# Narrow attention in 32-row products, with the last products of a step carried into the next

## The reference

```python
def _L0_xattn_ref(query, context, Wq, Wk, Wv, Wo):       # D_HEAD = 8, N_HEADS = 16
    Q = (query @ Wq.T).reshape(B, T_q, N_HEADS, D_HEAD)
    K = (context @ Wk.T).reshape(B, T_c, N_HEADS, D_HEAD)
    V = (context @ Wv.T).reshape(B, T_c, N_HEADS, D_HEAD)
    scores = jnp.einsum('bqhd,bkhd->bhqk', Q, K) / jnp.sqrt(8)
    attn = jax.nn.softmax(scores, axis=-1)
    return jnp.einsum('bhqk,bkhd->bqhd', attn, V).reshape(B, T_q, D) @ Wo.T
# _L2_xattn_ref: the same without the four weights (Q = query, K = V = context)
x = x + tanh(g_xattn[0]) * _L0_xattn_ref(layernorm(x), ctx, Wq, Wk, Wv, Wo)
x = x + tanh(g_ffn[0]) * _L0_ffn_ref(layernorm(x), ...)
x = x + tanh(g_xattn[1]) * _L1_xattn_ref(...)            # wide: 16 heads of 64
...
x = x + tanh(g_xattn[2]) * _L2_xattn_ref(layernorm(x), ctx, ctx)
...
```

## Time and profile before

| | us |
|---|---|
| time, median of 3 runs (lowest to highest) | 943.33 (939.79 to 945.34) |
| the profiled execution | 940.68 |
| its span, first to last instruction | 938.9 |
| PE matmul busy | 821.1 (87%) |
| DVE busy | 695.5 (74%) |
| ACT busy | 444.0 (47%) |
| POOL busy | 196.6 (21%) |

### The profile page before, as it was taken

One profiled execution on the slowest core, in us unless ns is written; L12 is line 12 of the kernel. 1 busy time (PEld: TensorE's weight loads), 2 busy tenths in 40 slices (PEclk: granted clock), 3 DMA queues, 4 the chain that ended last, 5 costly groups with the idle time before them and its releaser, 6 DMA issues. The chain is left out here.

```text
span 938.9 us, 14422 instructions
## 1 busy us (share of the span) xinstructions
PE 821.1 (87%) x5078; PEld 589.1 (63%) x5078; DVE 695.5 (74%) x1320; ACT 444.0 (47%) x663; POOL 196.6 (21%) x162
## 2 busy tenths in 40 slices
PE   4788878989999988999858887479999879999997
PEld 2555545667666677777646555346667567777774
DVE  6688866665766767888767888966766686887785
ACT  2245453224655514999514544145655225555553
POOL 2000010002365321222400001114554410111112
PEclk8699998987999998999968999779999989999999
DMA  9000000040101200000200060000222000000000
GB/s 363 13 1 0 1 1 1 1 179 1 42 7 46 46 1 1 1 1 0 90 0 1 1 285 1 1 1 2 46 46 47 1 1 1 0 1 0 0 1 23
DMA packets 3515, 29.48 MB, mean 31 GB/s; under 512 B 544, under 2 KB 768, under 8 KB 1920
## 3 DMA queue, kind: packets, MB, share of 16 engines
q1 hardware_dynamic: 3456, 28.70, 9.0%
HBM read 28.07 MB, written 0.62 MB: 31 GB/s over the span
## 5 line engine op out<-in xcount | busy, mean ns | idle before, releaser
L186 PE MATMUL banks<-normed_t_high,work_split 128*128 128x512 f32 x264 | 119.8, 454 | 15.5 <-DVE work L575 3.9
L889 POOL TENSOR_TENSOR work<-work 128x512 f32<-128x512 f32 x64 | 82.9, 1296 | 148.8 <-PE banks L745 106.7
L188 PE MATMUL banks<-normed_t_high,work_split 128*128 128x512 f32 x264 | 108.1, 410 | 0.0
L187 PE MATMUL banks<-normed_t_low,work_split 128*128 128x512 f32 x264 | 108.0, 409 | 0.0
L552 DVE TENSOR_REDUCE work<-banks 128x2 f32<-128x512 f32 x128 | 84.9, 687 | 27.3 <-PE banks L387 26.8
L499 ACT ACTIVATE work<-banks 128x1024 f32<-128x1024 f32 x64 | 65.3, 1024 | 47.9 <-PE banks L402 47.9
L186 PEld LDWEIGHTS banks<-normed_t_high,work_split 128*128 128x128 f32 x264 | 51.5, 195 | 37.8 <-issue 12.7
L1617 ACT ACTIVATE work<-banks 128x512 f32<-128x512 f32 x68 | 40.6, 597 | 72.1 <-PE banks L188 72.1
L1730 DVE TENSOR_TENSOR work<-work,banks 128x512 f32<-128x512 f32 x68 | 46.6, 686 | 35.3 <-ACT work L1617 34.8
L387 PE MATMUL banks<-work_split 128*128 128x256 f32 x256 | 61.0, 341 | 12.7 <-DVE work L552 10.1
L726 PE MATMUL banks<-work 128*64 128x256 f32 x512 | 69.4, 392 | 3.0 <-ACT work L856 1.7
(11 more groups left out here) (264 smaller groups left out, 1768.0 us busy)
## 6 DMA issues: line engine op xcount, KB each, us to landing
raw_b<-in_wf SPq DMA_DIRECT2D x1, 6528.0 KB, 18.1
raw_a<-in_wf SPq DMA_DIRECT2D x1, 4096.0 KB, 12.1
raw_b<-reciprocal_rows SPq DMA_DIRECT2D x6, 512.0 KB, 5.7
raw_a<-reciprocal_rows SPq DMA_DIRECT2D x6, 512.0 KB, 5.8
raw_a<-in_wf SPq DMA_DIRECT2D x1, 2048.0 KB, 13.6
raw_b<-in_wb SPq DMA_DIRECT2D x1, 2048.0 KB, 18.2
raw_a<-in_wb SPq DMA_DIRECT2D x1, 2048.0 KB, 7.3
small_operands<-in_small SPq DMA_DIRECT2D x1, 1530.0 KB, 9.1
```

The lines of the kernel that those rows point to most:

```text
L186: nc.tensor.matmul(o, w[0], m[0], start=start, stop=False)
L187: nc.tensor.matmul(o, w[0], m[1], start=False, stop=False)
L188: return nc.tensor.matmul(o, w[1], m[0], start=False, stop=stop)
L889: nc.gpsimd.tensor_tensor(w_ps[g % 2].rearrange("p (h q) -> p h q", h=2), v[:, :, 0, :], v[:, :, 1, :], ALU.add).then_inc(W["ps"].sem, 1)
```

## The change

- **Rows by selectors.** The three-term projection for each group and half is gone. In call 0 all heads are projected once, ahead of the first step (`small_project_pe`, four times `mm3`), and split into a high and a low part by ACT and DVE. In both calls `rows` then copies the 8 rows of each head of a group into their 32-row places by two products of 512 columns with matrices of zeros and ones (`a_selector`). ACT alone takes the result out of the bank (`stacked`), and adds the ones to the keys as the activation's bias. The DVE steps `stack`, `masked_keys` and the `small_weights` of each group are gone. The selectors come by two DMAs of 512 KB ahead of the bulk of the small operands (the two loads of 512 KB of repeated weights shrink to one of 128 KB), and ACT converts them to fp32r at the start of each call.
- **32-row products.** `maxima` and `scores` multiply only the 32 rows of a head (form 32 x 128), so the masked copies aren't needed. A group `u` of `scores` now covers two heads and both key halves of one batch, and its four products alternate between the two heads' row strips, into two banks; the two products of a `maxima` tile have the same head.
- **Order.** `values` goes by batch (eight products): the second batch of step `x` and the `sums_back` and `normalise` of step `x` stand inside step `x + 1`. The first batch stands behind the last `maxima`.
- **Constants.** `stream`, products of the identity with itself, stands at four places of a step of PE: nine products a step, and more ahead of the first step.
- All loops over the steps are written out. In call 1 the layernorm of the context (`context`) moves to the last step's place of the maxima on DVE, and `first_att` behind it. `sp` waits for other semaphores ahead of the loads of `wf1` and `wf3`.

```diff
-        A = signals("a", NG, w=2, q=4, hi=4, y=4, km=8, v=2, mx=16, red=16, m2=2, mt=2, yf=2, s=8, p=8, pv=8,
+        A = signals("a", NG, yp=4, y=4, v=2, mx=16, red=16, m2=2, mt=2, yf=2, s=8, p=8, pv=4,
...
+        def small_project_pe(pe):
+            pe.wait_ge(s_aw, 2)
+            for n in range(4):
+                h, k = n // 2, n % 2
...
+                mm3(bank(2 + n), [w[:, k * P:(k + 1) * P] for w in a_w], src).then_inc(s_aq, 1)
...
+            def rows(x, k):
...
+                elif k:
+                    at("y", 2 * x + 1)
+                else:
+                    at("att", x - 3)
+                hi, lo = (((xh, xl), (a_kh, a_kl)), ((xh, xl), (ch, cl)))[c][k]
+                nc.tensor.matmul(bank(a_bank(x, k)), a_selector(k, g, 0), half(hi, h), start=True, stop=False)
+                nc.tensor.matmul(bank(a_bank(x, k)), a_selector(k, g, 1), half(lo, h), start=False, stop=True)\
+                    .then_inc(A["yp"].sem, 1)
...
+            def maxima(x, n):
+                pair, j = n // GH, n % GH
...
+                at("red", 8 * x + n - 1)
+                for e in range(2):
+                    t = 4 * (x % 2) + 2 * pair + e
+                    last = nc.tensor.matmul(ps[:, 7 - n % 2, e * S:(e + 1) * S], a_y[a_rows(j), t * P:(t + 1) * P],
+                                            half(a_ky, x % 4)[a_rows(j), pair * S:(pair + 1) * S],
...
             def scores(x, u):
...
+                b = u // 2
+                at("p", 4 * x + u - 1)
+                for kb in range(2):
+                    for j in range(2 * (u % 2), 2 * (u % 2) + 2):
+                        last = nc.tensor.matmul(ps[:, j, kb * S:(kb + 1) * S],
+                                                half(a_ky, x % 4)[a_rows(j), b * S + kb * P:b * S + (kb + 1) * P],
+                                                half(a_yf, x % 2)[a_rows(j), b * S:(b + 1) * S],
...
+                more(0)
+                if x:
+                    stream(2, 4, S)
+                at("yf", x + 1)
                 scores(x, 0)
-                more(0, 1)
+                if x + 2 < STEPS:
+                    at("att", x - 1)
+                    stream(2)
+                next_rows(0)
+                more(1)
                 scores(x, 1)
                 more(2)
+                if x:
+                    values(x - 1, 1)
+                scores(x, 2)
                 more(3)
-                values(i, x, 0)
-                scores(x, 2)
-                if projecting:
-                    project(i, x + 2, 1)
+                if x + 2 < STEPS:
+                    at("y", 2 * (x + 2) + 1)
+                    stream(2)
+                next_rows(1)
                 more(4)
-                values(i, x, 1)
+                scores(x, 3)
                 more(5)
-                scores(x, 3)
+                if x:
+                    sums_back(x - 1)
                 more(6)
-                values(i, x, 2)
                 more(7)
-                values(i, x, 3)
...
+                values(x, 0)
+                if x + 1 < STEPS:
+                    stream(3, 4, S)
+                    maxima_back(x + 1)
...
+            for x in range(2):
+                rows(x, 0)
+                stream(3, 6)
+                rows(x, 1)
+                stream(3, 6)
             for n in range(8):
-                maxima(0, 0, n)
-            maxima_back(0, 0)
+                maxima(0, n)
+                stream(2)
+            stream(3)
+            maxima_back(0)
+            stream(4, 4)
```

The slots of ACT and of DVE, as they are now:

```diff
+            def slot(x):
+                weights(x, 0)
+                if x + 2 < STEPS:
+                    stacked(x + 2, 0)
+                weights(x, 1)
+                if x:
+                    sums(x - 1)
+                weights(x, 2)
+                if x + 2 < STEPS:
+                    stacked(x + 2, 1)
+                weights(x, 3)
...
+            def slot(x):
+                if x + 1 < STEPS:
+                    for n in range(8):
+                        largest(x + 1, n)
+                    minus(x + 1)
+                elif aside is not None:
+                    aside()
+                if x:
+                    normalise(x - 1)
+                if x + 1 < STEPS:
+                    queries(x + 1)
```

More of the change, by code:

```diff
@@ new lines, in small_project_act, with small_project_dve @@
+        def small_project_act(act):
+            for n in range(4):
+                act.wait_ge(s_aq, n + 1)
+                nc.scalar.activation(half((xh, a_kh)[n % 2], n // 2), bank(2 + n), ACT.Copy).then_inc(s_ah, 1)
+        def small_project_dve(dve):
+            for n in range(4):
+                dve.wait_ge(s_ah, n + 1)
+                hi, lo = ((xh, xl), (a_kh, a_kl))[n % 2]
+                nc.vector.tensor_tensor(half(lo, n // 2), bank(2 + n), half(hi, n // 2).bitcast(F32), ALU.subtract)\
+                    .then_inc(s_al, 1)
@@ new lines, in scores, with values @@
+                last.then_inc(A["s"].sem, 1)
+            def values(x, b):
+                if b == 0:
+                    at("v", x + 1)
+                    at("raw", x)
+                at("p", 4 * x + 2 * b + 2)
+                for kb in range(2):
+                    for j in range(GH):
+                        last = nc.tensor.matmul(ps[a_rows(j), 4, b * S:(b + 1) * S],
+                                                a_vg[:, 4 * (x % 2) + 2 * b + kb, j, :],
+                                                a_p[2 * b + j // 2][:, (2 * (j % 2) + kb) * S:(2 * (j % 2) + kb + 1) * S],
+                                                start=kb == 0, stop=kb == 1)
+                last.then_inc(A["pv"].sem, 1)
@@ L605, in small_dve, with slot @@
-            for x in range(2):
-                stack(0, x, 0)
-                stack(0, x, 1)
-                masked_keys(0, x)
-            small_weights(dve, c, 1, raw, r0)
+            def slot(x):
+                if x + 1 < STEPS:
[4 more added lines that the diff above has]
+                    aside()
+                if x:
+                    normalise(x - 1)
+                if x + 1 < STEPS:
+                    queries(x + 1)
@@ L610, in small_dve @@
             for n in range(8):
-                largest(0, 0, n)
+                largest(0, n)
             dve.wait_ge(s_ainit, c + 1)
-            minus(0, 0)
-            queries(0, 0)
-            with dve.Fori(0, NG - 2) as i:
-                order.loop(i, 4)
-                slot(i, 0, True, True, True)
-                slot(i, 1, True, True, True)
-            order.end(NG - 2)
-            slot(NG - 2, 0, True, True, True)
-            slot(NG - 2, 1, False, True, True)
-            slot(NG - 1, 0, False, False, True)
+            minus(0)
@@ L623, in small_dve @@
+            queries(0)
+            for x in range(STEPS):
+                slot(x)
             if before_last is not None:
                 before_last()
-            slot(NG - 1, 1, False, False, False)
+            normalise(STEPS - 1)
         def small_out_pe(pe):
@@ L1904, in context_and_first @@
                 norm_sums(dve, order, 6, 0, res)
-                for h in range(2):
-                    norm_tiles(dve, order, 5, h, ctok, ctok)
             def last_att(h):
```

329 lines of the change are left out of this document (147 added, 182 removed).

## The result

The changed kernel takes 915.19 us (median of 4 runs, 910.95 to 915.71), the kernel before 942.38 beside it: a ratio of 0.970, 95% interval 0.966 to 0.974. The profiled execution has a span of 913.0 us against 938.9. So 26 us were gained in the trace where 37.9 were forecast. Two runs of the kernels further down, one with all of the steps' constants on a strip (933.9 us) and one without the carry (966.4 us), were in a slower state at a lower granted clock; they count in the medians of the table there, but not in its ratios.

A forecast was written before the change was run, and what follows sets the result against it. DVE and PE were taken to hold each other up in a ring, neither full. Savings of 12.0 + 12.8 (steps) + 6.0 + 8.0 (starts) - 0.9 (ends) = 37.9 us took 940.7 to 903; range 878 to 930.

The forecast's parts named there:

- PE becomes the bound at 10.6 us a step: Steady steps: PE's list of products, constants and 13 form changes sums to 10.6 us, against 11.47 before.
- cheap changes: Rival, form changes: going between 32 rows and the full array costs nothing; 26 us less, 877; chance 0.14.
- no pairs: Rival, scores: 32-row products run one by one, costing 0.94 us more in 14 steps; 916; chance 0.12.
- dear changes: Rival, form changes: each costs 0.34 us, 2.2 more in 14 steps and 5 in the starts; 939; chance 0.06.
- open loads: Rival, maxima and scores: weight loads on one strip aren't hidden, 2.8 us a step; 942, no gain; chance 0.05.
- The starts, 6.0 and 8.0: Ahead of each call's first step: first queries come 6.0 us earlier in call 0 and 8.0 in call 1.
- Step 0 takes 8.3: First interval of each call: absent products and changes come off PE's list, 0.5 us wait for queries added; 8.3 us.
- The clock falls, as a rival: Rival, steps: 32-row products lower the clock, 8.3 us more a step; 1030, or 968 at half the time; chance 0.10.
- Constants mostly fill waits: Steps: most of the constants' 2.07 us isn't lost, since without them PE would wait about as long.
- No further wait: Steps: waits ahead of scores(x, 0) and maxima_back are covered by PE's other work, so 10.6 us stands.
- Ends of the calls, selectors and small operands: Call ends cost 0.9 us more together; selector copies fit ACT's idle time, and small operands' delay was taken as nothing.

The follow-up runs named there:

- all of the steps' constants on a strip: The filled kernel with all constants in the steps made 32-row products on strip 3, those ahead of the first step unchanged: 910.0 us, ratio 0.967.
- without the carry: The filled kernel with the last values and sums_back put back at the end of their own step, copy and normalise moved likewise: 960.9 us, ratio 1.023.
- the first experiment: The changed kernel with constants added in step 0 of each call, where later steps have other work: 911.1 us, ratio 0.968.
- the best kernel: The lean one, with step 0 filled, one pair of step constants on a strip, one moved and one dropped: 894.7 us, ratio 0.951.
- no constants in the steps: The changed kernel with all stream calls taken out of the steps, those ahead of the first step kept: 913.3 us, ratio 0.973.
- some constants on a strip: The changed kernel with constants between the first maxima and ahead of scores(x, 0) made 32-row products on strip 3: 906.0 us, ratio 0.965.
- the filled kernel: Same run as the first experiment: the changed kernel with nine more constants in step 0 of each call: 911.1 us, ratio 0.968.
- the one with moved constants: The filled kernel with the pair ahead of scores(x, 0) on a strip and the pair ahead of rows(x + 2, 1) moved before sums_back: 901.0 us, ratio 0.957.
- the lean one: The one with moved constants, also without the pair of constants ahead of rows(x + 2, 0): 894.7 us, ratio 0.951.
- the one with the second maximum first: The lean one with maxima(x + 1, 1) moved from behind the rows to ahead of scores(x, 0): 898.1 us, ratio 0.952.
- the bare start: The lean one without any constant ahead of the first step, those in the steps kept: 896.0 us, ratio 0.950.
- the short start: The lean one with, ahead of the first step, one constant for three behind each rows and one for two behind each maxima pair: 894.5 us, ratio 0.948.

## Why the prediction was right and where it was off

*PE becomes the bound at 10.6 us a step.* Right as to the bound: 10.44, with DVE idle for 3.8 us a step. That the number is so near is in part luck. The sum priced PE's work at 10.6 to 10.7, and it is 10.0, since `maxima` and `scores` on different strips run side by side (the rows from 62.62 on), about 0.6; the missed wait of 0.42 ahead of `sums_back` put most of it back. The prices held: pairs on two strips, loads hidden, 0.18 to 0.19 for a change of form. The rivals cheap changes, no pairs, dear changes and open loads are all out by the rows of 70.46 to 71.96. The total couldn't have told: 915 is what "no pairs" gave, 916. (The dear changes were also added up wrongly: thirteen changes a step, where the four to or from 32 columns had their price from rows.) The Trainium skill, TensorE: Matmul & The Clock Gate, Part 2, puts the last column's way through the array at about 128 cycles; with a change of form priced so, 9.1 us a step were estimated ahead. The 0.18 and 0.19 measured here are over three times that price, so that figure is not what a change costs. Its Part 3, by which loads overlap only where the row group differs, isn't borne out either: the pair of `maxima` at 70.46 has two weight loads on one strip and takes 0.23 us beside its change of form, so the second load isn't in the open.

*The starts, 6.0 and 8.0.* 5.5 and 7.5, at full clock as forecast. But constants that keep the clock aren't what shortens them: on the kernel before they bring 1.7 us of call 0, and without any the changed start is another 4.4 us shorter, with the clock falling in it. The gain is that of the order and of the projections and DVE steps that have left the start; the constants pay off only in the steps behind.

*Step 0 takes 8.3.* This is the term that failed, twice over. First its size: I took the absent products off PE's list without asking whether DVE keeps up. PE waits 0.55 and 0.76 for `largest`, 1.3 us that the sum doesn't have. As an estimate, the unfilled step at full clock would take 9.9: 6.65 to the end of the second wait, and 3.2 from there to `queries` as in a steady step (from its last four products of `maxima` at 67.35 to `queries` at 70.56). Even filled and at full clock the interval is 11.43, and 9.69 in the best kernel. Second, what it sets off: the clock at half, for 20.5 us in call 0 and 3.4 in call 1. Steps 0 and 1 of call 0 and step 0 of call 1 took 13.2 us more than forecast, and the first experiment took 6.9 of it back in the two steps of call 0 and 0.2 in step 0 of call 1 by filling. The rest of the 13.2 is the length of step 0 itself.

In all six calls whose step 0 isn't filled (the changed kernel, no constants in the steps, some constants on a strip) the clock fell in step 0. In none of the eight calls of the filled kernel, the one with moved constants, the lean one and the one with the second maximum first did it. The kernel with all of the steps' constants on a strip did so in one of its two. So, as far as the traces go, filling step 0 is what keeps the clock up there.

*The clock falls, as a rival.* I had put it on the 32-row products in all steps, with 8.3 more for one. (By its own prices 7.8 of the 10.6 us aren't 32-row products, not 6.8.) The step that was mostly at half clock costs 5.9 more (16.36 against 10.44): a product of 256 columns grows to 0.21 and not to 0.234, the wait ahead of `sums_back` isn't there, and the last 1.5 us of that step ran at full clock. The steady steps of this kernel hold the clock; the place at risk was step 0, the one stretch with gaps. I had asked the question for the stretch ahead of it (nothing there "leaves PE idle for long", and that held) and for the steps, but not for this one.

*Constants mostly fill waits.* Half right: 1.1 of 2.07 us. The two pairs ahead of the rows fill none.

*No further wait.* Not so: 0.42 ahead of `sums_back` in the full steps, some 4 us in all; moving one pair there won it back.

*The carry.* I gave it no price at all, and the gain hangs on it: with the rest of the order as it is, the kernel without it is slower than before.

*Ends of the calls, selectors and small operands.* 0.2 us more in all in place of 0.9; the first step's products started without a wait for the selectors. Nothing there moved the result.

What stays open: by what the chip decides to lower the clock. Idle PE goes ahead of it in the changed kernel, in the one without the carry and in the bare start, but with strips for constants, and in the short start, it fell with PE busy. Open too is why a fall lasts 3.4 us in one place and 20.5 in another behind the same gaps. And no run has the 32-row products or the selectors by themselves, with the order of the kernel before, so how the 26 us divide among these and the order isn't known beyond what the carry shows.

## What to carry to other kernels

When a software pipeline is made PE-bound, look at its first step, where the work carried over from a step before is missing: gaps there can cost the granted clock of the steps behind it, and here nine filler products in the gaps made the call 6.7 us shorter. Put such fillers where the trace shows PE waiting, one by one, and nowhere else: here seven a step cost nothing in waits, and one pair cost 0.45 us ahead of work that was ready. And ask of a filler what it buys: those ahead of the first step, removed, left the total where it was (896.0 against 894.7). Before praising the new operations, undo the reordering alone: here the carry was worth 2 us a step at full clock.

## What the runs showed of the hardware

- In the changed kernel the clock of 0.5 lasted from 38.1 to 58.6 us although PE was busy for 20.37 of these 20.50 us, and in the bare start for 34 us (22.6 to 56.7). Here being busy again didn't bring it back at once. Behind the same two waits in call 1 it lasted 3.4 us.
- In the start with strips the clock fell at 25.1 us with PE busy for 3.94 of the 4.07 us before it, when part of its constants used 32 rows; in the short start, whose constants are on all rows, it fell at 24.9 us with no wait of PE from 13.6 us on.
- Products on different strips run side by side even where they belong to different groups: `maxima` and `scores`, eight products in 0.51 us without the change of form, where 0.70 would be their sum.
- A change between 128 rows, 32 rows and 32 columns cost 0.17 to 0.19 us each way; two 32-row products on one strip took as long as four on two strips (0.42 and 0.43 us with the change).
- At half clock a PE-bound step didn't take twice as long: 15.16 us at a mean clock of 0.51 in the bare start, against 9.45 in the lean kernel.
